# Stores of the last stage of a graph network, issued by ScalarE in place of SyncE

## The reference, cut to what matters

```python
x = _layernorm(x + _L0_gnn_ref(x, edge_weight, W, b, edge_index), axis=-1)
x = _layernorm(x + _L1_gnn_ref(x, src, dst, edge_attr_20, edge_weight, edge_attr_3, ...), axis=-1)
```

```python
S = agg[:, :2 * F] @ (W1_s / np.sqrt(2 * F))    # done before this stage
S = shifted_softplus(S)
S = S @ (W2_s / np.sqrt(C))
```

## Time and profile before

| what | value |
|---|---|
| median of three executions | 1063.95 us |
| the profiled execution's own time | 1060.8 us |
| its span | 1058.7 us |
| TensorE clock granted, mean | 0.965 |
| first load of the last stage issued | 949.11 us |
| end of the last stage | 1058.7 us |
| PE / DVE / ACT / POOL busy over the whole span | 89% / 79% / 66% / 61% |
| DMA over the whole span | 265 GB/s |

### The profile page before, as it was taken

How to read it: one execution, slowest core, us unless ns; L and a number is a source line. 1 busy time by engine, 2 the same in 40 slices (tenths; PEclk the granted TensorE clock), 3 DMA queues, 4 the chain that set the end, 5 groups by cost and what they waited for, 6 DMA issues and landing times.

```text
span 1058.7 us, 17984 instructions
## 1 busy us (share of the span) xinstructions
PE 943.4 (89%) x5218; PEld 767.6 (73%) x5218; DVE 837.9 (79%) x2368; ACT 703.7 (66%) x1641; POOL 642.6 (61%) x931
## 2 busy tenths in 40 slices
PE   5979999898894999999999679999999999929885
PEld 4958777776673788888888457887888888818774
DVE  5778788887662789888888758888888888817998
ACT  2668877787682466666666645666666666618997
POOL 4017888888863356666666354676666766534664
PEclk9989999999896999999999889999999999969998
DMA  9989999999998599988999586999999999768999
GB/s 346 418 303 223 247 238 237 237 238 238 231 236 192 217 321 331 331 318 318 334 327 331 223 295 166 220 227 213 206 222 229 215 206 218 122 102 329 410 416 365
DMA packets 105703, 280.43 MB, mean 265 GB/s; under 512 B 13107, under 2 KB 17479, under 8 KB 105607
## 3 DMA queue, kind: packets, MB, share of 16 engines
q1 hardware_dynamic: 68598, 191.42, 49.3%
q0 software_dynamic: 35280, 82.63, 40.7%
q10 hardware_dynamic: 1728, 5.24, 1.3%
HBM read 132.38 MB, written 146.87 MB: 264 GB/s over the span
## 4 chain that ended last, share of the span: by engine, by line
PE 55%; DMA 6%; DVE 5%; issue 2%; ACT 1%; POOL 1%; SPq 0%; DVEq 0%; POOLq 0%; ACTq 0%
PE bank L1330 14%; PE bank L1334 7%; PE bank L1378 7%; PE bank L1361 7%; PE bank L1392 5%; PE bank L1390 3%; PE bank L1321 3%; PE bank L1355 3%; DVE stat L1168 2%; PE bank L1388 2%; PE bank L1367 2%; DMA out<-R_mem 1%; DMA sum<-R_mem,l_sidx 1%; PE bank L1365 1%; PE bank L1356 1%
## 5 line engine op out<-in xcount | busy, mean ns | idle before, releaser
L552 POOL DMA_INDIRECT sum<-R_mem,sidx_all x79 | 131.3, 1662 | 91.1 <-DMA sum<-zeros 49.3
L613 POOL DMA_INDIRECT sum<-R_mem,l_sidx x79 | 134.6, 1704 | 48.3 <-DMA sum<-R_mem,l_sidx 25.3
L1330 PE MATMUL bank<-G_hi 128*128 128x512 f32 x316 | 130.4, 413 | 0.0
L599 POOL DMA_INDIRECT G_mem<-x_d,dst_i x79 | 77.3, 979 | 87.3 <-PE bank L1365 61.5
L1330 PE MATMUL bank<-G_lo,G_hi 128*128 128x512 f32 x316 | 124.2, 393 | 0.0
L1244 PE MATMUL bank<-G_hi,M_mem 128*128 128x512 f32 x200 | 85.4, 427 | 9.4 <-ACT R_mem L685 9.4
L1334 PE MATMUL bank<-G_hi,G_lo 128*128 128x512 f32 x316 | 85.3, 392 | 0.0
L1119 DVE SCALAR_TENSOR_TENSOR edge_mem<-edge_mem,Y,bank 128x128 f32<-128x128 f32 x237 | 71.2, 385 | 15.1 <-ACT edge_mem L806 14.1
L1361 PE MATMUL bank<-edge_mem,Winv 128*128 128x512 f32 x158 | 81.8, 600 | 0.1
L1244 PE MATMUL bank<-G_lo,M_mem 128*128 128x512 f32 x200 | 79.6, 398 | 0.0
L1255 PE MATMUL bank<-edge_mem,Wf_s 128*128 128x256 f32 x320 | 78.6, 390 | 0.7 <-ACT node_mem L679 0.7
(11 more groups left out here) (263 smaller groups left out, 2921.2 us busy)
## 6 DMA issues: line engine op xcount, KB each, us to landing
node_mem<-sum SPq DMA_DIRECT2D x41, 512.0 KB, 5.9
filt_d<-node_mem SPq DMA_DIRECT2D x40, 512.0 KB
node_mem<-filt_d SPq DMA_DIRECT2D x79, 256.0 KB
sum<-zeros SPq DMA_DIRECT2D x33, 512.0 KB
G_mem<-x SPq DMA_DIRECT2D x20, 512.0 KB, 6.3
x_d<-node_mem SPq DMA_DIRECT2D x20, 512.0 KB, 2.9
sum<-node_mem SPq DMA_DIRECT2D x20, 512.0 KB, 4.5
edge_mem<-x SPq DMA_DIRECT2D x19, 512.0 KB, 6.3
```

Source lines behind the costliest of these rows:

```text
L552: pool.indirect_dma_start(sum0, bass.IndirectOffsetOnAxis(ap=sidx[:, t:t + 1], axis=0), R[t % 8][:, :], None, compute_op=ALU.add).then_inc ...
L599: pool.indirect_dma_start(G3[t % 8][:, :], None, x1_d, bass.IndirectOffsetOnAxis(ap=dst_i[:, t:t + 1], axis=0)) \
L613: pool.indirect_dma_start(sum1, bass.IndirectOffsetOnAxis(ap=l1_sidx[0:n, t:t + 1], axis=0), R3[t % 8][0:n, :], None, compute_op=ALU.add). ...
L1330: pe.matmul(bank[4 + a][:, :], zT_hi[a][:, c * P:(c + 1) * P], w[c][:, :], start=(c == 0 and w is W0h), stop=False)
```

## The change

SyncE's loop keeps the loads and their wait. The stores go to ScalarE, behind line 865 of the step in which the first half of the pair is finished, each with a wait for `g_y1` and one for `g_y0`. The helper `pairs_in` moves up so that both programs can use it. The semaphores that the stores count up, and SyncE's last wait for all stores, stay.

```diff
-            for s in range(T2 + NA - 3):
-                if s < T2:
-                    if s >= NA:
-                        sp_.wait_ge(rows_st[(s - NA) % 8], SUM1 + 16 * ((s - NA) // 8 + 1))
-                    sp_.dma_start(pairs_in(al[s % NA], s), node_pair(sum1, s, 0, D)).then_inc(g_al[s % NA], 16)
-                if s >= NA - 3:
-                    t = s - NA + 3
-                    sp_.wait_ge(g_y0, t + 1)
-                    sp_.wait_ge(g_y1, t + 1)
-                    sp_.dma_start(node_pair(out, t, 0, D), pairs_in(al[t % NA], t)).then_inc(rows_st[t % 8], 16)
+            for s in range(T2):
+                if s >= NA:
+                    sp_.wait_ge(rows_st[(s - NA) % 8], SUM1 + 16 * ((s - NA) // 8 + 1))
+                sp_.dma_start(pairs_in(al[s % NA], s), node_pair(sum1, s, 0, D)).then_inc(g_al[s % NA], 16)
...
                     act.activation(al[b][:, 0, :], al[b][:, 0, :], ACT.Identity, bias=tiny4[a][:, 6, 0:1],
                                    scale=tiny4[a][:, 5, 0:1]).then_inc(g_y0, 1)
+                    act.wait_ge(g_y1, t + 1)
+                    act.wait_ge(g_y0, t + 1)
+                    act.dma_start(node_pair(out, t, 0, D), pairs_in(al[b], t)).then_inc(rows_st[t % 8], 16)
```

More of the change, by code:

```diff
@@ L395, in build, with pairs_in @@
         minus = before[:, 0:P]
+        def pairs_in(tile, s):
+            return tile[:, :, :] if s < T2 - 1 else tile[0:N - s * 256, 0:1, :]
         block = ctx.enter_context(nc.Block())
@@ L507, in _ @@
             sp_.wait_ge(f_scat, 16 * TR)
-            def pairs_in(tile, s):
-                return tile[:, :, :] if s < T2 - 1 else tile[0:N - s * 256, 0:1, :]
-            for s in range(T2 + NA - 3):
-                if s < T2:
-                    if s >= NA:
-                        sp_.wait_ge(rows_st[(s - NA) % 8], SUM1 + 16 * ((s - NA) // 8 + 1))
-                    sp_.dma_start(pairs_in(al[s % NA], s), node_pair(sum1, s, 0, D)).then_inc(g_al[s % NA], 16)
-                if s >= NA - 3:
-                    t = s - NA + 3
-                    sp_.wait_ge(g_y0, t + 1)
-                    sp_.wait_ge(g_y1, t + 1)
-                    sp_.dma_start(node_pair(out, t, 0, D), pairs_in(al[t % NA], t)).then_inc(rows_st[t % 8], 16)
+            for s in range(T2):
+                if s >= NA:
+                    sp_.wait_ge(rows_st[(s - NA) % 8], SUM1 + 16 * ((s - NA) // 8 + 1))
+                sp_.dma_start(pairs_in(al[s % NA], s), node_pair(sum1, s, 0, D)).then_inc(g_al[s % NA], 16)
             for v in range(8):
```

## The result

The changed kernel took 1078.16 us (median of four runs, 1075.15 to 1082.29), the kernel before 1063.45 us (median of four, 1062.75 to 1065.17). The ratio is 1.0143, with a 95% interval of 1.0115 to 1.0171: slower, by about 15 us (14.7 us between the medians, 15.2 us by the ratio). The forecast was 1081 us, in a range of 1075 to 1089.

A forecast was written before the change was run, and what follows sets the result against it. ScalarE, VectorE and the DMA engines were taken as full at once, with ScalarE the only bound after the change. 15.0 + 0.5 + 1.2 = 16.7 us on 1063.95 us gave 1081 us, range 1075 to 1089.

The forecast's parts named there:

- ScalarE's exposed wait and issue: ScalarE, start of line 865 to start of 869: 1.24 us in place of 0.71 us, 0.53 us more a step.
- ScalarE's step without a gap: Last stage: ScalarE's own work of 2.31 us a step becomes 2.84 us, the only bound.
- The sum: Last stage: 15.0 us over 33 steps, 0.5 us for the issue in the first, 1.2 us at the end: 16.7 us.
- The end: Six pairs finished after the last line 869: 1.2 us more, with the last store costing the same from either queue.
- The mean step: Kernel before, 33 steps of the last stage: 2.385 us each, 2.31 us ScalarE's work and 0.075 us waits.
- The signs: Changed profile: steps 2.8 to 2.9 us, issues 0.33 to 0.44 us, VectorE waiting about 0.5 us a step, some 370 GB/s.
- The wait for `g_y1`: ScalarE ahead of each store: costs nothing, as VectorE's line 1163 is a microsecond ahead.
- The freed loads: SyncE's loads no longer behind stores: at most ScalarE's waits vanish, 33 x 0.075 = 2.5 us.
- The hidden issue: Rival: the store's issue runs beside line 865 or 869, leaving only the 2.5 us gain, 1061.5 us; chance 0.04.
- The dear and colliding issues: Rivals on ScalarE's issue: 1.35 us each, 1115 us, chance 0.04; or colliding with SyncE's loads, mean 0.66 us, 1091 us, 0.11.

The follow-up runs named there:

- the first experiment: Changed kernel with each ScalarE store being that of the pair finished one step earlier, its waits met long before: 1060.32 us against 1059.49 us before, ratio 1.0005.

## Why the prediction was right

*ScalarE's exposed wait and issue.* This was the step that carried the forecast, and the experiments confirm it: wait or issue alone cost the kernel nothing that can be measured, together they cost 15 us. I had 0.53 us a step; it is 0.57 us. The issue is 0.34 and not 0.38 us. The way to it is 0.08 and not 0.03 us: I read it from a SyncE store whose last-met wait was not the separate one. The restart is 0.05 and not 0.03 us.

*ScalarE's step without a gap.* I took 2.31 us from the earlier trace rows. The changed kernel's 2.80 us less 0.57 us leave 2.23 us, and the step of 2.40 us with the store behind the logarithm less its 0.16 us leaves 2.24 us. The steps of 2.31 us before held 0.08 us of waiting that no row reports as idle: the copy and the absolute value start 0.33 us apart in them (1011.34 to 1011.67), and 0.25 us apart now (1002.01 to 1002.26 above). The kernel before had shown it: its first and its last of the 33 steps take 2.22 us. What held the others was TensorE: the absolute value starts at 1011.67 when TensorE's line 1409 ends at 1011.64, and TensorE had waited in that step for VectorE's line 1159. VectorE had no gap, so I take it to have set the pace, but no run tried it. The 0.04 us too little for wait and issue and the 0.08 us too much for the step nearly cancel, which is luck: 2.84 us forecast, 2.80 us measured.

*The sum.* The 33 steps brought 92.54 - 78.72 = 13.8 us (15.0 forecast). From the first load to the first of them there are 20.66 us in place of 19.48 us, 1.2 us more (0.5 forecast); the other two profiles of the changed kernel have 20.2 and 19.9 us, so part of this varies from run to run. Behind the last logarithm (1066.10 and 1047.31) there are 12.0 us in place of 11.4 us, 0.6 us more (1.2 forecast). Together 15.6 us against 16.7 us. The end holds two things. Up to the start of the last scale-and-shift (1075.15 and 1055.29) it is 1.1 us longer, near the 1.2 us forecast. From there to the end of the span it is 2.95 us in place of 3.41 us. The forecast had the last store, of 32 KB, at the same cost from either queue. It landed 2.1 us after the issue on SyncE and 1.6 us after that on ScalarE (last number of the row):

```profile
out<-edge_mem SPq DMA_DIRECT2D x1, 32.0 KB, 2.1
```

```profile
out<-edge_mem ACTq DMA_DIRECT2D x1, 32.0 KB, 1.6
```

The same shows in the other profiles: 2.9 to 3.0 us with the last store alone behind the last scale-and-shift on ScalarE, 3.4 us with SyncE.

*The mean step.* I read 2.385 us as 2.31 us of work and 0.075 us of waits in every step. It is a mean of shorter steps and five long ones near the end, at the pace of the DMA queues (2.58 us in the forecast's own reading). With 2.80 us a step both lie inside, so the sum did not suffer.

*The signs.* The middle of the stage moved 369 GB/s, as forecast (some 370). VectorE's new wait for the logarithm was 12.1 us over 33 steps, under 0.4 us a step and not 0.5 us.

*The wait for `g_y1`.* It was forecast to be free. The logarithm's idle time is put down to the scale-and-shift of ScalarE in all 33 steps and never to VectorE.

*The freed loads.* They were bounded at 2.5 us, a bound that rested on the 2.31 us (with 2.23 us it would have been 5.1 us), and were worth nothing, for a reason I had not given: not that nobody waits for the data, but that the ring of 14 buffers is full.

*The rivals.* The hidden issue is real, as the first experiment shows, but needs waits that are met early enough. The advice of the Trainium skill ("Perfetto Trace Analysis", section "DMA Optimizations") to give loads to one engine and stores to another won nothing here even with the issue hidden. The dear and colliding issues did not occur: of the changed kernel's 40 stores none took over 0.375 us.

## What to carry to other kernels

On ScalarE here an issue was free while earlier instructions of the engine still ran, and was paid in full (0.57 us a step with its wait) when it had to wait for the end of the instruction right ahead of it. So issue the result of an earlier step there, or put an instruction that can start at once between the producer and the store. Look at the steps one by one and not only at their mean, which can hide two different limits. Before a queue is split, look whether the waits in it ever held up data that somebody needed: here the loads were late only near the end, at the pace of full DMA queues, and a full ring of buffers would have taken the gain back anyway.

## What was not expected of the hardware

- Of two waits ahead of an issue the one written second became an instruction of its own, some 0.06 us when it was met last; the order of the two was worth 0.05 us a step.
- An issue right behind another on ScalarE took 0.46 us where a lone one took 0.34 us.
- An engine without reported idle time can still be paced by others: ScalarE's rows showed nothing, and its step was 0.08 us longer than its own work.
- An issue on ScalarE started 0.09 to 0.10 us behind the moment at which the last wait of a compute instruction ahead of it was met, and did not wait for these instructions to run (three cases, in the kernels that store one step later and behind the next absolute value).
- The last store, 32 KB, landed 0.5 us sooner after an issue by ScalarE than after one by SyncE. No run shows why.
